# One-core layer stack: sum of squares in another bank, four output-weight remainders on VectorE, and the output product behind the intra product in the last chunks

## The reference, cut to what matters

```
proj = x_normed @ in_proj_w.T              # gate, conv input, dt
xBC  = silu(causal conv with 4 taps + bias)  # x, B, C
state = state * dA_t + dtx_t * B_t ;  y_t = state @ C_t   # per token and head
y  = y + x * D
yn = y * rsqrt(mean(y*y over the 512 channels of a group) + 1e-5) * norm_weight * silu(gate)
out = yn @ out_proj_w.T                    # summed over groups, added to the residual x
```

## Time and profile before

| | |
|---|---|
| median of 3 runs | 1316.47 us (1316.01 to 1316.78) |
| the profiled execution | 1317.65 us, its span 1315.8 us |
| PE busy | 1233.3 us, 94% of the span |
| VE, ACT, POOL busy | 933.4, 694.3, 693.2 us |
| mean granted PE clock | 0.977 |
| mixer groups, first transposes of chunk 0 | group 0 at 61.36, group 4 at 523.84, group 7 at 872.00 us |
| last group's chunk 4, first transposes | 932.03 us |

### The profile page before, as it was taken

How to read it: one execution, slowest core, us unless ns; L and a number is a source line. 1 busy time by engine, 2 the same in 40 slices (tenths; PEclk the granted TensorE clock), 3 DMA queues, 4 the chain that set the end, 5 groups by cost and what they waited for, 6 DMA issues and landing times.

```text
span 1315.8 us, 21907 instructions
## 1 busy us (share of the span) xinstructions
PE 1233.3 (94%) x6690; PEld 968.5 (74%) x6690; DVE 933.4 (71%) x1718; ACT 694.3 (53%) x1042; POOL 693.2 (53%) x739
## 2 busy tenths in 40 slices
PE   5999999999999999999999999999879999889976
PEld 4777777787777777777777777777657777667754
DVE  5786677668767766776776677668776555469995
ACT  3666666566666756665676667665423333222220
POOL 5067566656655665665565566564663443333330
PEclk9999999999999999999999999999889999889996
DMA  5111021011102101100210110010103232221100
GB/s 176 46 50 34 2 66 34 18 34 49 33 1 65 33 17 33 49 26 7 64 33 17 33 49 25 9 38 1 33 18 117 92 92 88 72 67 39 53 17 25
DMA packets 44233, 57.52 MB, mean 44 GB/s; under 512 B 10117, under 2 KB 21159, under 8 KB 43929
## 3 DMA queue, kind: packets, MB, share of 16 engines
q1 hardware_dynamic: 44185, 56.92, 14.3%
HBM read 49.95 MB, written 6.96 MB: 43 GB/s over the span
## 4 chain that ended last, share of the span: by engine, by line
PE 68%; DVE 12%; issue 7%; ACT 6%; POOL 5%; DMA 1%; DVEq 0%; ACTq 0%; POOLq 0%; SPq 0%
PE p_tile L94 11%; PE p_gate L94 8%; PE p_d L94 7%; PE p_tile L98 5%; PE p_y L1134 4%; DVE conv L718 4%; PE p_gate L98 4%; PE p_d L98 3%; PE p_in L1113 3%; PE p_x L1121 2%; PE t_p_a L1883 2%; PE p_y L94 2%; PE t_p_c L1951 1%; PE p_d L1090 1%; PE p_x L1070 1%
## 5 line engine op out<-in xcount | busy, mean ns | idle before, releaser
L718 DVE SCALAR_TENSOR_TENSOR conv<-p_tile,conv_taps,conv 128x511 f32<-128x511 f32 x189 | 141.4, 748 | 50.4 <-ACT conv L597 35.4
L652 ACT ACTIVATE squares<-y 128x512 f32<-128x512 f32 x64 | 40.5, 633 | 154.5 <-DVE y L865 124.5
L828 DVE TENSOR_TENSOR em<-em,p_gb 128x512 f32<-128x512 f32 x128 | 82.2, 683 | 52.7 <-ACT em L631 52.2
L94 PE MATMUL p_tile<-xn_hi,wc_hi 128*128 128x512 f32 x252 | 109.9, 436 | 9.4 <-ACT gate_second L618 8.6
L530 POOL TENSOR_TENSOR squares<-squares 128x256 f32<-128x256 f32 x64 | 47.1, 736 | 113.2 <-ACT squares L652 113.2
L94 PE MATMUL p_tile<-xn_lo,wc_hi 128*128 128x512 f32 x252 | 98.5, 391 | 0.0
L718 DVE SCALAR_TENSOR_TENSOR conv<-p_gate,conv_taps,conv 128x511 f32<-128x511 f32 (+2 forms) x90 | 66.7, 742 | 44.6 <-ACT conv L597 44.4
L498 POOL TENSOR_TENSOR x_w<-xs,head_g 128x512 f32<-128x512 f32 x56 | 59.0, 1053 | 72.0 <-ACT xs L627 69.8
L738 DVE TENSOR_TENSOR zt_lo<-p_y,zt_hi 128x512 fp32r<-128x512 f32 x63 | 43.6, 692 | 71.7 <-ACT zt_hi L607 71.7
L602 ACT ACTIVATE xbc<-conv 128x512 f32<-128x512 f32 x96 | 60.7, 632 | 63.1 <-DVE conv L726 40.8
L94 PE MATMUL p_d<-wr_hi,zt_hi 128*128 128x512 f32 x236 | 93.8, 397 | 0.1
(11 more groups left out here) (391 smaller groups left out, 3675.4 us busy)
## 6 DMA issues: line engine op xcount, KB each, us to landing
w_raw<-w SPq DMA_DIRECT2D x108, 256.0 KB, 2.7
q_words<-q SPq DMA_DIRECT2D x33, 256.0 KB, 2.6
h_ring<-h_lo_rows SPq DMA_DIRECT2D x6, 704.0 KB, 4.8
h_lo_rows<-h_rest SPq DMA_DIRECT2D x11, 256.0 KB, 2.0
x_res<-x SPq DMA_DIRECT2D x8, 256.0 KB, 5.0
out<-out_t SPq DMA_DIRECT2D x8, 256.0 KB, 2.2
h_lo_rows<-h_rest SPq DMA_DIRECT2D x11, 128.0 KB, 1.9
gate_second<-w SPq DMA_DIRECT2D x4, 256.0 KB, 5.3
```

The costliest lines, as they stand in the source:

```text
L94: pe.matmul(out, lhs(k)[0], rhs(k)[n], start=(start and k == 0 and n == 0), stop=False)
L718: ve.scalar_tensor_tensor(out=conv[:, s, sh:], in0=p[:, 0:HALF - sh], scalar=conv_w[:, bass.ds(g, 1), j, tap], in1=conv[:, s, sh:], op0=AL ...
L828: ve.tensor_tensor(m, m, gm.unsqueeze(1).broadcast_to([P, HG // 2, P]), ALU.mult)\
```

## The change

Seven edits. (1) The sum of squares goes to the last columns of `p_d1`, the second decay bank (to `p_gb` in the tail); `sum_rows` waits for both exponentials of its chunk, the decay product of a chunk for the variance of the chunk two before, and the intra product for `s_zlo` in place of `s_v`. (2) `out_rest` is gone: all four remainders of the output weights are one VE instruction each, and ACT rounds them in order. (3) In chunk 0 ACT's `gate_silu` stands ahead of the wait for y and the squares. (4) VE does taps 1 and 2 of the second tile ahead of `z_rest`. (5) In the tail PE does the intra product first, then `sum_rows` and `out_product`; VE's `variance` stands behind y times gate, `residual` and `row_stats` behind `z_rest`. (6) POOL's `norm` stands behind the addition to y there, and `sum_squares` and `rstd_of` are in another order. (7) After chunk 7 the first `spread` waits for the exponentials alone, the second for the last but one residual. In the diff "..." marks lines left out; empty lines of context are left out too.

```diff
@@ -235,9 +235,9 @@
-    def ss_bank(c):
-
-        return (p_y if c < NC else p_gb)[:, 3 * P:3 * P + 1]
+    def ss_bank(last, c):
+
+        return (p_gb if last and c >= CH else p_d1)[:, 3 * P:3 * P + 1]
@@ -256,10 +256,9 @@
     OUT = TILES + KT
-    VE_LO = [OUT, OUT + 1]
-    POOL_LO = list(range(OUT)) + ["scaled", OUT + 2, "scaled", OUT + 3]
-    FIRST = [0, 1, 2, 3, 6, 7, 8, 9, 4, 5] + POOL_LO[OUT:]
-    ROUNDED = [OUT + 2, OUT + 3, OUT, OUT + 1]
+    VE_LO = list(range(OUT, WT))
+    POOL_LO = list(range(OUT))
+    FIRST = [0, 1, 2, 3, 6, 7, 8, 9, 4, 5]
@@ -274,9 +273,7 @@
-        if w >= OUT:
-            return g * WT + OUT + ROUNDED.index(w) + 1
-        return g * WT + (FIRST.index(w) if is_zero(g) else w) + 1
+        return g * WT + (FIRST.index(w) if is_zero(g) and w < OUT else w) + 1
@@ -445,7 +442,7 @@
             sp.wait_ge(s_z, (G - 1) * NC + CH)
-            for w in (VE_LO[-1], WT - 1):
+            for w in (WT - 1, TILES - 1):
                 sp.wait_ge(*lo_count(G - 1, w))
@@ -479,17 +476,17 @@
                 st = g * (NC - 1) + c
-                if last and c >= CH:
-                    sum_squares(n - 1)
-                if last and c > 1:
+                if last and 1 < c < CH:
                     rstd_of(c - 2)
...
                         .then_inc(s_std, 1)
-                if not (isinstance(g, int) and n == 0) and not (last and c >= CH):
+                if not (isinstance(g, int) and n == 0):
                     sum_squares(n - 1)
+                if last and c >= CH:
+                    rstd_of(c - 2)
                 if c == 0:
@@ -509,17 +506,15 @@
                     small_operands()
-                if c == 0:
-                    out_rest(g, OUT + 2)
-                if not (isinstance(g, int) and n == 0):
+                if not (isinstance(g, int) and n == 0) and not (last and c >= CH):
                     norm(n - 1, (c - 1) % 2)
-                if c == 0:
-                    out_rest(g, OUT + 3)
                 if c > 0:
...
                     pool.tensor_tensor(y[:], y[:], x_d[:], ALU.add).then_inc(s_txd, 1)
+                if last and c >= CH:
+                    norm(n - 1, (c - 1) % 2)
                 if last and c == CH + 1:
@@ -547,16 +542,6 @@
                 .then_inc(s_wlo, 1)
-
-        def out_rest(g, w):
-
-            raw = w_raw[:, w % RAW, :]
-            scale = norm_w[:, bass.ds(g, 1), w - OUT].broadcast_to([P, D])
-            pool.wait_ge(s_whi, hi_count(g, w))
-            pool.tensor_tensor(raw, raw, scale, ALU.mult).then_inc(s_wlo, 1)
-            done, count = lo_count(g, w)
-            pool.wait_ge(done, count - 1)
-            pool.tensor_tensor(lo_of(w), raw, hi_of(w).bitcast(F32), ALU.subtract).then_inc(s_wlo, 1)
@@ -564,15 +549,15 @@
             pool.tensor_tensor(rstd[:, c:c + 1], rstd[:, c:c + 1], m_half[:], ALU.pow).then_inc(ln_rs, 1)
-        for w in FIRST[:OUT]:
+        for w in FIRST:
             w_rest(0, w)
...
         group(G - 1, True)
+        sum_squares(LAST)
         rstd_of(NC - 2)
-        sum_squares(LAST)
         up.rest(pool, 0, 0, 0)
@@ -641,17 +626,19 @@
                     wait(act, s_out, n)
-                    for w in ROUNDED:
+                    for w in range(OUT, WT):
                         w_round(g, w)
...
                     tile_in(T, tg, j)
+                made = gate_tile(g, last, c)
+                if c == 0:
+                    gate_silu(CH + n, made[1], made[2], gate_bank(c))
                 act.wait_ge(s_y, n + 1)
...
                 act.activation(squares[:], y[:], ACT.Square).then_inc(s_sq, 1)
-                made = gate_tile(g, last, c)
-                if made and c % CH < 2:
+                if made and 0 < c % CH < 2 or made and c == CH:
                     gate_silu(CH + n, made[1], made[2], gate_bank(c))
@@ -664,7 +651,7 @@
                 w_round(0, c - CH)
-        for w in FIRST[CH:OUT]:
+        for w in FIRST[CH:]:
             w_round(0, w)
@@ -818,7 +805,7 @@
                 for tile in left:
-                    tile_taps(*tile, range(2, TAPPED[tile[3]]))
+                    tile_taps(*tile, range(3, TAPPED[tile[3]]))
                 for k in rows_in(last, c):
@@ -829,11 +816,8 @@
                     tile_taps(*tile, range(TAPPED[tile[3]]))
-                if not first:
-                    variance(n - 1, (c - 1) % 2, ss_bank(c))
-                if tail:
-                    residual(n - 1, c - 1, out_bank(last, c))
-                    row_stats(c - 1)
+                if not first and not tail:
+                    variance(n - 1, (c - 1) % 2, ss_bank(last, c))
                 if c > 0:
@@ -872,9 +856,16 @@
                     .then_inc(s_z, 1)
+                for tile in later:
+                    tile_taps(*tile, range(1, 3))
+                if tail:
+                    variance(n - 1, (c - 1) % 2, ss_bank(last, c))
                 if last and c == NC - 1:
...
                 z_rest(n, p)
+                if tail:
+                    residual(n - 1, c - 1, out_bank(last, c))
+                    row_stats(c - 1)
                 if last and c == 2:
@@ -885,8 +876,6 @@
                     up.unpack(ve, 0, 1)
-                for tile in later:
-                    tile_taps(*tile, range(1, 2))
@@ -977,7 +966,7 @@
         row_norm(NC - 2)
-        variance(LAST, (NC - 1) % 2, ss_bank(NC))
+        variance(LAST, (NC - 1) % 2, ss_bank(True, NC))
         up.scale(ve, 0, 1, 1)
@@ -1070,6 +1059,8 @@
                 wait(pe, s_m, 2 * n)
+                if tail:
+                    pe.wait_ge(s_v, n - 1)
                 if c % CH == 0:
@@ -1081,7 +1072,8 @@
                 wait(pe, s_e, 2 * n)
-                wait(pe, s_res, n - 1)
+                wait(pe, s_res, n - 2 if tail and c > CH else n - 1)
+                wait(pe, s_v, n - 1)
                 if first:
@@ -1094,15 +1086,12 @@
                     pe.wait_ge(s_whi, (g + 1) * WT)
-                    for w in (VE_LO[-1], WT - 1):
-                        pe.wait_ge(*lo_count(g, w))
-                if not first:
-                    if tail:
-                        pe.wait_ge(s_sg, LAST + 1)
-                    else:
-                        pe.wait_ge(s_e, 2 * n + 1)
+                    pe.wait_ge(*lo_count(g, WT - 1))
+                if not first and not tail:
+                    pe.wait_ge(s_e, 2 * n + 1)
                     out_product(n - 1, out_bank(last, c))
-                    sum_rows(n - 1, ss_bank(c))
+                    pe.wait_ge(s_e, 2 * (n + 1))
+                    sum_rows(n - 1, ss_bank(last, c))
                 for k in rows_in(last, c):
@@ -1128,12 +1117,16 @@
                 else:
-                    wait(pe, s_v, n)
+                    wait(pe, s_zlo, n)
                 for h in range(HG):
...
                 mm.then_inc(s_intra, 1)
+                if tail:
+                    sum_rows(n - 1, ss_bank(last, c))
+                    pe.wait_ge(s_sg, LAST + 1)
+                    out_product(n - 1, out_bank(last, c))
                 next_gate(g, last, n, c)
@@ -1172,11 +1165,13 @@
         group(G - 1, True)
-        pe.wait_ge(s_res, LAST)
+        pe.wait_ge(s_e, 2 * (LAST + 1))
         up.spread(pe, 0, 0, 0)
         pe.wait_ge(l2_lo, NC - 2)
+        pe.wait_ge(s_res, LAST)
+        pe.wait_ge(s_v, LAST)
         up.spread(pe, 0, 1, 1)
-        sum_rows(LAST, ss_bank(NC))
+        sum_rows(LAST, ss_bank(True, NC))
         out_product(LAST, p_y)
...
         up.product(pe, 0, 0, 0)
```

## The result

The changed kernel takes 1304.68 us (median of 4 runs, 1302.44 to 1305.03) beside 1316.62 us of the kernel before on the same chip: a ratio of 0.990, 95% interval 0.9888 to 0.9915. It is faster, by 11.9 us where 27.0 were forecast, and lies above the range of 1284.5 to 1300. The profiled execution took 1304.97 us, its span is 1303.2 us, so the traces differ by 1315.8-1303.2 = 12.6 us.

A forecast was written before the change was run, and what follows sets the result against it. PE, busy 94% of the span, was taken to bound the mixer before the tail, and a loop through all engines the tail. Group 0 3.4 + looped groups 18.8 + group 7 3.8 + tail 1.0 = 27.0 us, giving 1289.5 us, range 1284.5 to 1300.

The forecast's parts named there:

- the tail: Edits 5 to 7, last group from chunk 4: 4.9 us less at full clock, 2.6 more with it fallen; booked 1.0 less.
- the dear end: Tail with the clock fallen after each of four waits, at 1.7 us a stretch: 2.6 us more than before.
- Rival D: The tail loses: 1289.5+3.6 = 1293.1 us; chance 0.11.
- Looped groups: Six looped groups, edits 1 and 3: chunks 0, 1, 2, 7 give 0.33, 1.74, 0.83, 0.24 us; 18.8 us in all.
- The cost is nothing on PE: Edit 2, looped groups: four remainders on VE at 4.0 us cost PE nothing; at 7.1 us, 1 us a group.
- Edit 2 on VE: Chunk 0: four remainders take 4.0 us, three taps towards 0.7 us together, y comes about 1 us earlier.
- Group 0: Gives 3.4 us: the 1.70 us wait for a VE tap, and another 1.74 in chunks 1 and 2.
- rival B: Looped groups: another wait replaces the one removed, through late z or VE work; about half kept, 1300 us; chance 0.16.
- Group 7's chunks 0 to 3: Chunk 2 falls from 16.77 to 12.96 us: 2.20 of waiting and the rest half clock; booked 3.8 us.
- Rival C: The tail at full clock: 1289.5-3.9 = 1285.6 us; chance 0.11.
- E: Slower: VE bounds the looped groups, four remainders meet POOL (7.1 us) and delay y in chunk 0; 1321.6 us; chance 0.03.
- the signs I listed: Group 4 chunks of 14.6, 15.7, 13.0 us, `w_rest` mostly 0.74 us, tail idle ahead of row transposes, loops 11 to 12 us.

The follow-up runs named there:

- bank_alone: The kernel before with edit 1 alone, outside the tail: sum of squares in the second decay bank, no wait for the variance; 1316.11 us (one run).
- wrest_late: The changed kernel with VE's four remainders of the output weights behind `z_rest` of chunk 0 instead of ahead of y; 1345.3 us, ratio 1.022.
- wrest_mid: The changed kernel with VE's four remainders behind z, ahead of chunk 0's later taps, instead of ahead of y; 1307.29 us, ratio 0.993.
- silu_back: The changed kernel with edit 3 alone undone, so the gate's Silu stands behind the squares again in chunk 0; 1305.33 us, ratio 0.991.
- filler: The changed kernel with unread matmuls ahead of the first row transposes of chunks 4 to 7 and the second spread; 1292.75 us, ratio 0.981.

## Why the prediction was wrong

**The step that failed** is the tail: "At 2.4 GHz throughout I get 4.9 us less for the tail; with the clock fallen after each of four waits 2.6 us more." Forecast between 62.0 and 69.5 us and booked at 65.9, it took 77.5. Two terms of it were mis-sized. The price of the clock was 2.6+4.9 = 7.5 us for the case that came, and measured 11.3: I had one stretch of 3.42 us at 1.7 us for each of four waits, while the record has 27.3 us of half clock in the tail. The stretch from 956.4 lasts 10.2 us and covers most of the output product at 962.76, that from 970.0 lasts 6.8 us and covers nearly all of the one at 972.28, and nothing hides either product. (4 x 1.7 is 6.8 us; the prediction does not say where the other 0.7 of its 7.5 is from.) And its tail at full clock was 4.1 us too short, 62.0 against 66.1. The third part of the 11.6 us was a choice: 3.6 us from the middle that I booked to the dear end (3.6+3.8+4.1 = 11.5). The loops that I put at 10.7 and 11.5 us, without listing the steps that add up to them, take 12.0, 12.6 and 12.2 at full clock, and chunk 4 waits 3.81 us where I wrote "2 to 3". The loop has POOL's steps in it: in chunk 6 the row norm stands idle behind POOL's memsets. VE's timeline of the changed kernel:

```profile
941.93 1.25 DVE L757 TENSOR_SCALAR h_rest<-x_res,mean_var,rstd 128x512 f32<-128x512 f32 x1 [1.01 <-POOL rstd L533]
```

I named the cover that goes and the fall of the clock, and then took a gain of 1.0 us, "nearer the middle". Rows 9 and 10 were evidence for the dear end: the clock had fallen after 2.20 us, and every wait I listed was about as long. Rival D was the right mechanism, but it put 3.6 us on the forecast (1293.1 us) where 11.6 came in the tail.

**The clock after a wait.** Three of the tail's four waits for the row norm were longer than the "2 to 3 us" that I expected (3.81, 4.52 and 4.99 us), but half clock followed the wait of 2.71 us ahead of 927.83 too, and one of 1.70 us in `bank_alone`. The Trainium skill, in TensorE: Matmul & The Clock Gate, section HAM oscillation, which I weighed, ties the fall to gaps longer than I expected in the tail. The three longer waits do not speak against its rule; the waits of 2.71 and 1.70 us do, as by it the mixer of `bank_alone` would have kept its clock. Where the page and these rows differ, the rows decide.

**Looped groups**, 3.1 us a group forecast, 18.4/6 = 3.1 measured. The size was right, partly by luck, and one reason was wrong. Chunk 1 gave 1.50 us of its 1.74, and chunk 3, for which nothing was booked, 0.11. Edit 3 does not remove chunk 1's wait; edit 2 does, by bringing y of chunk 0 forward. "The cost is nothing on PE", I wrote of edit 2, and booked no gain for it; alone it gives 9.9 of the 18.4 us.

**Edit 2 on VE.** VE's timeline of the changed kernel, chunk 0 of group 4:

```profile
521.46 0.73 DVE L713 SCALAR_TENSOR_TENSOR conv<-halo,conv_taps,conv 128x3 f32<-128x3 f32 x3
...
522.90 3.51 DVE L743 SCALAR_TENSOR_TENSOR wr_lo<-w_raw,norm_scale,wr_hi 128x512 fp32r<-128x512 f32 x4
...
527.66 0.67 DVE L854 TENSOR_TENSOR y<-x_d,p_y 128x512 f32<-128x512 f32 x1
```

Four remainders in 3.51 us (4.0 forecast), three taps in 0.73 (0.7 forecast). y starts 0.26 us before chunk 1 where it started 539.81-538.76 = 1.05 us into it: 1.3 us earlier, 1 forecast. Four took 3.51 us beside one POOL instruction (`state_dec`) and 5.12 us in `wrest_late` beside three (`x_w`, `x_dt`, `x_d`). In `wrest_mid` they took 3.43 us beside three others, and it was POOL that lost: the second fold of the squares took 0.80 us instead of 0.47, `x_w` 1.50 instead of 1.05. The Trainium skill says, in SBUF — State Buffer, section Who interferes with whom, that a VectorE instruction with two SBUF inputs and a GpSimd one that reads SBUF contend, and that the order of issue decides which is blocked. These rows agree in that either engine can be the one that loses; what decides between them they do not show.

**Group 0** gave 1.8 us of 3.4. The tap's 1.70 came: chunk 0 fell from 75.74-61.36 = 14.38 us to 12.64. The other 1.74, booked because group 7 does the same work faster, did not: chunks 1 and 2 take 30.36 us beside 30.41. PE and ACT of the changed kernel in that chunk 1:

```profile
80.23 0.47 PE L94 MATMUL p_d<-wr_hi,zt_hi 128*128 128x512 f32 x1 [1.45 <-ACT em L616]
```

```profile
76.25 0.63 ACT L640 ACTIVATE squares<-y 128x512 f32<-128x512 f32 x1 [1.01 <-DVE y L854]
...
78.09 1.28 ACT L616 ACT_TABLE_LOAD   x1
79.38 1.09 ACT L616 ACTIVATE em<-p_d 128x512 f32<-128x512 f32 x2
```

The output product overwrites a decay bank that ACT's exponential still reads, and that exponential stands behind y, the squares, z's rounding and a table load. Chunk 0 of group 0 is shorter for PE (11.80 us busy, 14.62 in group 4) and not for ACT (9.79 and 9.70), and VE reaches y 1.1 us into chunk 1, not 0.26 ahead of it. They are late there: the wait of 1.45 us takes the place of those that were removed (0.62 us for `p_tile` in chunk 1 and 0.47 us for the variance in chunk 2), rival B, in one group of eight.

**Group 7's chunks 0 to 3**: 3.4 us of 3.8. Chunk 2 gave 3.8; chunk 1 gave 0.3 back (16.04 against 15.71), which by `silu_back` is edit 3's.

**The rest.** Rival C, the full clock, is not what came, but `filler` makes it at 1292.75 us, not 1285.6. E, that VE bounds the looped groups, did not come in this form, and `wrest_late`, 2% slower than before, shows what it looks like. Of the signs I listed, the chunk windows, the lack of waits on `ssv` and the 0.74 us remainders came as written, and so did the idle ahead of the row transposes; loops of 13.6 to 14.4 us instead of 11 to 12 were the sign that the forecast was wrong.

One thing stays open: why the same 1.70 us wait drew the clock down in five looped groups and not in group 2, with PE busy throughout ahead of it in all six. No run was made for it.

## What to carry to other kernels

An order that only moves PE's idle time is not neutral: ask what PE does in the wait and what stands behind it, and price a fallen clock by the serial PE work that follows, not by the shortest stretch seen (7.5 us forecast here, 11.3 measured). Where a wait can't go, matmuls that nobody reads, put ahead of the wait, can be worth more than the reordering (here 11.9 us). And test edits that free the same loop together as well as alone: two worth 0 and 9.9 us alone were, with two small ones, worth 18.4.

## What the runs showed of the hardware

- The granted clock fell to 0.50 after waits of 1.70 us (`bank_alone`, groups 1 and 3 to 6) and 2.71 us, stayed up after the same 1.70 us in group 2, and stayed up in `filler` through waits of 1.78 and 2.24 us that stood behind unread matmuls. PE's timeline of `filler` at chunk 7:

```profile
949.64 0.39 PE L1025 MATMUL p_tile<-wr_hi 128*128 128x512 f32 x1
952.26 0.66 PE L1042 MATMUL p_tile<-identity,h_rest 128*128 128x128 f32 x4 [2.24 <-DVE h_rest L757]
```

  The length of one wait does not settle it. What else does, these runs do not show: PE was busy without a break ahead of the wait in group 2 and in the other five alike.
- Unread matmuls cost nothing where PE would have waited: the 12 at 909.32 take 3.10 us, and the row transposes behind them start 5.39 us into the chunk, as without them.
- The row norm for one tile (L757), which reads one large operand, took 0.55 us alone at 983.69 and 1.25 us at 941.93, where POOL was forming `x_w`, and again 1.25 us at 956.34 beside `x_dt`: not only instructions with two large inputs are stretched.
